# One block for first FFN and projection, transposes moved into the fourth lookup unit, split indices, and the second FFN's first norm spread over the scan

## The chip, the cores and the metric

The kernel runs on one core of a Trainium2 chip. The metric is the device time in microseconds of one execution, the median of several runs. Beside it stands one profiled execution, with its own time and span.

## The reference

A macaron layer on x of 2048 tokens by 256 channels, fp32: half an FFN, a Mamba-2 block, half an FFN.

```
x = x + 0.5 * ffn(layernorm(x))
x = x + mamba(layernorm(x))
x = x + 0.5 * ffn(layernorm(x))
```

The FFN (both times the same weights) takes its three matrices from a table of 16 values by index: `w = lut[idx]` for gate and up (688 x 256) and down (256 x 688), then `silu(gate) * up` and down. The Mamba block is

```
proj = h @ in_proj_w * mup            # z 512, xBC 768, dt 64
xBC  = silu(conv4(xBC) + conv_b)      # causal, 4 taps, by channel
dt   = softplus(dt + dt_bias); dA = exp(-dt * exp(A_log))
state = state * dA + dtx (x) B;  y = C . state   # 2048 steps, 64 heads of 8, state 128
y = (y + D * x); out = rmsnorm(y) * norm_w * silu(z) @ out_proj_w
```

## The kernel before

Tokens are cut in 16 tiles of 128; four tiles make a group (`GT`, `GROUPS` = 4). fp32 products are made of three float32r matmuls of high and low parts (`split_mm`, L68 to L70). There are three stages, each written as a block in which the five engines have their own programs; at a block's end all engines wait for each other.

**build_front** first makes the FFN's weights. A unit is a quarter of the gate and up indices (64 rows, the low table entries' masks on partitions 0 to 63 and the high ones' on 64 to 127, 1408 columns). For each of seven entry pairs VectorE compares the indices with the entry (`mask_d`, L256), ScalarE makes the eighth mask, and TensorE multiplies each mask by a diagonal of table values, three matmuls over 512, 512 and 384 columns (`lookup`, L420), eight masks adding up to the weights in PSUM, which ScalarE copies out (`evac`). Four such units (`QTR`) are followed by six for the down matrix (`low_d`, 512 columns), interleaved with the first group's FFN. The masks of the down units share memory with those of the first four, so VectorE starts them when the fourth unit's last lookup is done (`aused_ok`). Index DMAs are issued on SP's queue (partitions 0 to 63) and on ScalarE's (64 to 127), a quarter each; SP then issues the activations (`x_res`), the down indices and the projection's weights (`win_raw`, `wout_raw`).

The layer norm is the class **Norm**: VectorE computes statistics of a group (`dve_stats`: four `bn_stats`, four `bn_aggr`, one add of eps), GpSimd the inverse root by `pow` (`pool_rstd`, tile `n_rstd`), VectorE the normalised rows (`dve_xn`, tile `n_xn`), TensorE eight transposes (`pe_transpose`, L529), ScalarE the high and VectorE the low parts (`act_hi`, `dve_lo`, tile `n_xT`). For group 0 the statistics stand on VectorE behind the third unit's masks, the rows behind two masks of the fourth, and the transposes on TensorE between third and fourth unit.

Then come four groups of FFN: hidden chunks, then `product` sums into `f_down`, and VectorE adds the result to `x_res` (L317). In the meantime GpSimd subtracts to get the low parts of the projection's weights (`win`, L231) and, at the end, of the output weights (`wout`, L239). The latter stand behind three `pool_rstd` in its queue; the last of these waits for the statistics of group 2 of the projection's norm.

**build_in_proj** is the projection, by group in 11 chunks, six matmuls each, into four PSUM banks `pj` (the memory of the FFN's gate and up banks). ScalarE copies a chunk out (`pre`, `cv`, `zs`), VectorE does three convolution taps for each of six chunks (L643), GpSimd carries the last columns over. `cv`, `zs`, `xbd`, `w` and the others of `mamba_t` lie where the first FFN's weights and raw indices were. VectorE's program begins with the scaling of `conv_w` and `norm.dve_stats(dve, LAST)`.

**build_scan** has 18 steps: in step c it prepares tile c, multiplies tile c-1 and finishes tile c-2 (names a, b_, z; `do_a`, `do_b`, `do_z`). On VectorE a step is, in this order: `xdt` (L1151), `yf`, `u`, `ssum`, two masked products (`mmat`, L1127), the parts of `y` and `state`, a third `mmat`, the update of `x_res` by the output product (L1234, which waits for GpSimd's root `rstd_y`), `y` (L1239) and a fourth `mmat`. GpSimd computes `gs`, `tmp`, `uh`, the weighted inputs `w` (L1274) and `rstd_y`. TensorE's segment products are `seg` (L859, L864), its transposes of `y` L954. At the 48th `yf` (tile 11) SP issues the DMAs that read the FFN's weights back from DRAM. The norm of the second FFN's group 0 stands at the end: statistics of group 0 behind step a = 14, its root on GpSimd at the end of that step, the rows behind step 15 (a = `LAST`); the statistics of group 1 stand inside the last step (z = `LAST`), between the second and third hidden chunk of the FFN's first group.

Of the kernel before, what the change touches and what calls it, by code (L numbers as in the profile page):

```python
# [19 lines left out]
F32 = mybir.dt.float32  # L20
# [105 lines left out]
def build_front(nc, T, A, norm):  # L126
# [3 lines left out]
    with ExitStack() as ctx:  # L130
        sb = lambda n, s, d=F32: ctx.enter_context(nc.sbuf_tensor(n, s, d))
        ps = lambda n, s: ctx.enter_context(nc.psum_tensor(n, s, F32))
        sem = lambda n: ctx.enter_context(nc.semaphore(n))
# [6 lines left out]
        W = GUC * P  # L140
        with ExitStack() as first:
            big = lambda n: first.enter_context(nc.sbuf_tensor(n, [P, W], F32R))
            mask_d, mask_a = [big(f"mask_d{n}") for n in range(GU_D)], [big(f"mask_a{n}") for n in range(GU_A)]
# [10 lines left out]
            "vec_in", "x0_in", "x_in", "win_in", "wout_in", "gu_in0", "gu_in1", "gu_in2", "gu_in3"))  # L154
        dn_in, ident_ok, half_ok, entry_ok, zeroed, hz, two_ok, lut_ok, table_ok = map(sem, (
# [4 lines left out]
            "gate_ok", "up_ok", "silu_ok", "h_ok", "h_hi", "h_lo", "down_ok", "res_ok", "stored"))  # L160
        win, wout, wgu, wd, x_res = T["win"], T["wout"], T["wgu"], T["wd"], T["x_res"]
# [36 lines left out]
        def _(pool):  # L198
# [26 lines left out]
            for k in range(KC):  # L225
# [3 lines left out]
                for part in range(4):  # L229
                    c = slice(part * PCH * P // 4, (part + 1) * PCH * P // 4)  # L230
                    pool.tensor_tensor(win[:, 1, k, :, :].rearrange("p c n -> p (c n)")[:, c], win_raw[:, k, c],  # L231
                                       win[:, 0, k, :, :].rearrange("p c n -> p (c n)")[:, c].bitcast(F32), ALU.subtract)
            norm.pool_rstd(pool, GROUPS)
            norm.pool_rstd(pool, GROUPS + 1)
            norm.pool_rstd(pool, GROUPS + 2)
            pool.wait_ge(h_lo, GROUPS * FCH)
            pool.wait_ge(split_hi, KC + 1)
            for k in range(4):
                pool.tensor_tensor(wout[:, 1, k, :], wout_raw[:, k, :], wout[:, 0, k, :].bitcast(F32), ALU.subtract)  # L239

        @block.vector
        def _(dve):
            def masks(unit, first=1, end=PAIRS):
                for p in range(first, end):
# [5 lines left out]
                    else:  # L250
# [4 lines left out]
                        src = dn_idx[:, 2 * d:2 * d + halves, :].rearrange("p a c -> p (a c)")  # L255
                    dve.tensor_scalar(dst, src, entry[:, p:p + 1], None, ALU.is_equal).then_inc(mask_ok, 1)  # L256
# [15 lines left out]
            norm.dve_start(dve)  # L272
            for unit in range(QTR - 1):
# [46 lines left out]
        def _(act):  # L320
            for q in range(QTR):
# [32 lines left out]
            act.wait_ge(entry_ok, 2 * PAIRS + 4)  # L354
            for unit in range(2):
# [1057 lines left out]
```

## Time and profile before

| | us |
|---|---|
| median of 3 runs | 511.39 |
| lowest, highest run | 511.18, 514.34 |
| profiled execution, its time | 512.58 |
| its span | 510.7 |
| TensorE busy | 470.6 (92%) |
| VectorE busy | 375.0 (73%) |
| ScalarE, GpSimd busy | 280.0, 160.1 |

Terms of the profile: PE is TensorE (PEld its weight loads), DVE VectorE, ACT ScalarE, POOL GpSimd, SP SyncE. A row of the timeline has its start, its length, the engine, the line of the kernel, the operation with output and inputs, and the number merged in it. In brackets behind it stands how long the engine had been idle and what ended that; "issue" is a wait for nothing that the profile shows. `PEq` is TensorE's sequencer. PEclk is the granted clock of TensorE, 1.00 for 2.4 GHz and 0.50 for 1.2 GHz.

### The profile page before, as it was taken

The numbers are of one execution on the slowest core, as the hardware profiler recorded it, in microseconds if no ns is written. First come the engines' busy times: TensorE is split into PE (matmuls) and PEld (weight loads), VectorE is DVE, ScalarE is ACT, GpSimd is POOL, SyncE is SP. The second block draws the span as 40 slices with busy tenths as digits, with TensorE's granted clock in tenths as the row PEclk, the third lists the DMA queues.
The fourth block names the chain that finished last, engine by engine and source line by source line (L and its number), as shares of the span: only waits on it lengthen the run. The fifth ranks groups of instructions, "written<-read, shape, count | busy, mean of one in ns | idle before, by whom it ended". The sixth has DMA issues, their size and how long they took to land.

```text
span 510.7 us, 17071 instructions
## 1 busy us (share of the span) xinstructions
PE 470.6 (92%) x7454; PEld 396.2 (78%) x7454; DVE 375.0 (73%) x745; ACT 280.0 (55%) x505; POOL 160.1 (31%) x215
## 2 busy tenths in 40 slices
PE   3979999999989999888899999999978999999997
PEld 3766798888888787766787788878857778898987
DVE  6977954656678999975788888888759766556443
ACT  3639644344327899998566656666545433323241
POOL 1010032203023111116666667667546310000000
PEclk9979999999999999899999999999989999999999
DMA  8940052000000000010000000000530000100001
GB/s 215 258 187 1 0 227 124 0 3 0 1 0 1 2 1 0 22 42 4 5 5 4 4 6 4 6 4 6 190 167 5 4 1 0 42 20 22 22 21 41
DMA packets 7226, 21.29 MB, mean 42 GB/s; under 512 B 752, under 2 KB 5360, under 8 KB 6512
## 3 DMA queue, kind: packets, MB, share of 16 engines
q1 hardware_dynamic: 6752, 18.05, 10.4%
q10 hardware_dynamic: 400, 2.16, 1.7%
q8 instruction: 58, 0.95, 0.8%
q14 instruction: 16, 0.13, 0.1%
HBM read 12.87 MB, written 6.55 MB: 38 GB/s over the span
## 4 chain that ended last, share of the span: by engine, by line
PE 37%; issue 7%; ACT 4%; POOL 3%; DVE 3%; POOLq 0%; DVEq 0%; ACTq 0%
PE intra L886 5%; PE seg L864 3%; PE yo L1008 2%; POOL w L1274 2%; PE seg L859 1%; PE XB L938 1%; PE new L989 1%; PE yo L954 1%; PE XB L974 1%; PE yo L1011 1%; PE prior L984 1%; PE XB L68 1%; PE yo L70 1%; PE yo L69 1%; PE yo L68 1%
## 5 line engine op out<-in xcount | busy, mean ns | idle before, releaser
L1274 POOL TENSOR_TENSOR w<-xdt,ends 32x512 f32<-32x512 f32 (+3 forms) x63 | 66.5, 1073 | 3.7 <-ACT seg L1035 2.3
L643 DVE SCALAR_TENSOR_TENSOR cv<-pre,vec,cv 128x512 f32<-128x512 f32 x72 | 52.9, 750 | 2.5 <-ACT cv L684 0.8
L514 POOL TENSOR_TENSOR n_rstd<-n_ve,m_half 128x4 f32<-128x4 f32 x12 | 13.0, 1086 | 125.7 <-DVE n_ve L509 125.6
L1035 ACT ACTIVATE seg<-seg 128x512 f32<-128x512 f32 x64 | 35.9, 579 | 29.2 <-PE seg L864 29.1
L1127 DVE TENSOR_TENSOR mmat<-seg,gs 128x512 f32<-128x512 f32 x64 | 42.4, 685 | 9.3 <-ACT seg L1035 8.9
L68 PE MATMUL pj<-n_xT,win 128*128 128x512 f32 x88 | 35.3, 401 | 4.8 <-ACT cv L684 2.4
L864 PEld LDWEIGHTS seg<-abk,m_seg 96*32 96x32 bf16 x2048 | 20.7, 96 | 24.2 <-DVE mmat L1127 13.7
L1048 ACT ACTIVATE f_hT<-f_h 128x512 fp32r<-128x512 f32 (+1 forms) x24 | 15.2, 632 | 40.2 <-DVE f_h L1138 40.2
L70 PE MATMUL pj<-n_xT,win 128*128 128x512 f32 x88 | 34.8, 395 | 0.0
L864 PE MATMUL seg<-abk,m_seg 96*32 96x64 bf16 x2048 | 27.0, 195 | 8.4 <-issue 5.6
L69 PE MATMUL pj<-n_xT,win 128*128 128x512 f32 x88 | 34.6, 393 | 0.0
L1297 POOL TENSOR_TENSOR uh<-u,uh 128x512 fp32r<-128x512 f32 x16 | 21.0, 1312 | 42.0 <-ACT uh L1089 40.2
L378 ACT ACTIVATE f_hT<-f_h 128x512 fp32r<-128x512 f32 (+1 forms) x24 | 15.2, 632 | 34.5 <-DVE f_h L297 34.4
L1142 DVE TENSOR_TENSOR f_hT<-f_h,f_hT 128x512 fp32r<-128x512 f32 (+1 forms) x24 | 16.6, 692 | 16.8 <-ACT f_hT L1048 16.8
L301 DVE TENSOR_TENSOR f_hT<-f_h,f_hT 128x512 fp32r<-128x512 f32 (+1 forms) x24 | 16.5, 689 | 14.0 <-ACT f_hT L378 14.0
L256 DVE TENSOR_SCALAR mask_d<-gu_idx,entry 128x1408 fp32r<-128x1408 int32 x28 | 24.4, 948 | 2.3 <-DMA gu_idx<-in_gu 2.3
L374 ACT ACTIVATE f_sg<-f_gate 128x512 f32<-128x512 f32 (+1 forms) x24 | 14.1, 587 | 19.2 <-PE f_gate L70 19.1
L68 PEld LDWEIGHTS pj<-n_xT,win 128*128 128x128 f32 x88 | 16.7, 189 | 9.4 <-ACT cv L684 3.8
L68 PE MATMUL f_down<-wd,f_hT 128*128 128x256 f32 x80 | 23.0, 288 | 0.3 <-ACT wd L351 0.3
L69 PE MATMUL f_down<-wd,f_hT 128*128 128x256 f32 x80 | 22.7, 283 | 0.0
L70 PE MATMUL f_down<-wd,f_hT 128*128 128x256 f32 x80 | 22.6, 283 | 0.0
L1165 DVE SCALAR_TENSOR_TENSOR yf<-cv,vec,yo 128x128 f32<-128x128 f32 x64 | 18.0, 343 | 5.2 <-PE yo L954 5.2
(266 smaller groups left out, 1448.7 us busy)
## 6 DMA issues: line engine op xcount, KB each, us to landing
wgu_dram<-wgu SPq DMA_DIRECT2D x1, 2816.0 KB, 8.2
wgu<-wgu_dram SPq DMA_DIRECT2D x1, 2816.0 KB, 10.5
out<-x_res SPq DMA_DIRECT2D x8, 256.0 KB, 2.1
x_res<-in_x SPq DMA_DIRECT2D x1, 1536.0 KB, 22.5
wd_dram<-wd SPq DMA_DIRECT2D x1, 1536.0 KB, 11.6
wd<-wd_dram SPq DMA_DIRECT2D x1, 1536.0 KB, 13.6
gu_idx<-in_gu ACTq DMA_DIRECT2D x4, 352.0 KB, 8.3
gu_idx<-in_gu SPq DMA_DIRECT2D x4, 352.0 KB, 9.5
```

The costliest lines, as they stand in the source:

```text
L68: pe.matmul(out, w_hi, x_hi, start=start, stop=False)
L69: pe.matmul(out, w_hi, x_lo, start=False, stop=False)
L70: return pe.matmul(out, w_lo, x_hi, start=False, stop=stop)
L256: dve.tensor_scalar(dst, src, entry[:, p:p + 1], None, ALU.is_equal).then_inc(mask_ok, 1)
L643: dve.scalar_tensor_tensor(dst, pre[:, x, k:k + GN].rearrange("p (t c) -> p t c", c=P), cw[:, x, k:k + 1], dst, ALU.mult, ALU.add).then_in ...
L864: ins = pe.matmul(out[Q * b:Q * b + Q, i, :], T["m_seg"][:, IU * (n - 1) + i, :], T["abk"][:, b, a, :], start=True, stop=True)
L886: ins = pe.matmul(intra[Q * g:Q * g + Q, :, hh, :], mmat[b_ % 2][:, :, h], xbd[b_ % 2][:, h, :, :], start=True, stop=True)
L1035: act.activation(seg[u_ % 2][:, :, :], seg[u_ % 2][:, :, :], ACT.Exp).then_inc(s["exp_ok"], 1)
L1127: dve.tensor_tensor(mmat[a % 2][:, i, :], seg[u_ % 2][:, :, :], gs[a % 2][:, i].unsqueeze(2).broadcast_to([P, IU, HEADS]), ALU.mult).then_ ...
L1165: dve.scalar_tensor_tensor(yf[:, P * g:P * g + P].rearrange("p (b t) -> p b t", b=NB), cv[:, z, g, :].rearrange("p (b t) -> p b t", b=NB), ...
L1274: pool.tensor_tensor(heads(w[r, n, :]), heads(xdt[a % 2][r, :]), ends[a % 2][r, n * HEADS:(n + 1) * HEADS].unsqueeze(2) .broadcast_to([Q * ...
L1297: pool.tensor_tensor(uh[:, 1, :, :].rearrange("p g t -> p (g t)"), u[:, :], uh[:, 0, :, :].bitcast(F32).rearrange("p g t -> p (g t)"), ALU ...
```

## The change

- The block that holds the first FFN also holds the projection. Where the block's end separated them, the projection's VectorE, ScalarE and GpSimd programs wait at their start for all that reads the memory that they write (`ffn1_places`: the last `down_ok`, all subtractions, the weights' stores to DRAM), and TensorE waits for `win`. GpSimd's `wout` subtractions now stand ahead of the last `pool_rstd` of the front.
- The first unit's indices come in two pieces, of 512 and 896 columns, on both queues. VectorE makes the first 512 columns of three masks from the first piece; TensorE waits for both parts of each such mask.
- Group 0's transposes stand behind three of the fourth unit's eight lookups.
- The second FFN's statistics of group 0 are done one tile a step (steps 6 to 9, the end in step 10), those of group 1 in steps 11 to 14 with the end in step 15, the rows of group 0 one tile a step in steps 12 to 15. All of these stand between the third `mmat` and the update of `x_res`. GpSimd's root for group 0 moves from step 14 to step 11.

```diff
@@ build_front
+        T["ffn1_read"] = ((down_ok, GROUPS * GT // 2), (split_lo, 4 * KC + 4), (stored, 32))
+        T["ffn1_banks"], T["win_parts"] = (res_ok, GROUPS * GT // 2), ((split_hi, KC), (split_lo, 4 * KC))
-        block = ctx.enter_context(nc.Block())
@@ sync
-            sp.dma_start(gu_idx[0:H64, 0, :], A["gu"][:, 0, :]).then_inc(gu_in[0], 16)
+            sp.dma_start(gu_idx[0:H64, 0, 0:GN], A["gu"][:, 0, 0:GN]).then_inc(gu_first, 16)
+            sp.dma_start(gu_idx[0:H64, 0, GN:], A["gu"][:, 0, GN:]).then_inc(gu_in[0], 16)
@@ gpsimd
             norm.pool_rstd(pool, GROUPS)
             norm.pool_rstd(pool, GROUPS + 1)
-            norm.pool_rstd(pool, GROUPS + 2)
             pool.wait_ge(h_lo, GROUPS * FCH)
             pool.wait_ge(split_hi, KC + 1)
             for k in range(4):
-                pool.tensor_tensor(wout[:, 1, k, :], wout_raw[:, k, :], wout[:, 0, k, :].bitcast(F32), ALU.subtract)
+                pool.tensor_tensor(wout[:, 1, k, :], wout_raw[:, k, :], wout[:, 0, k, :].bitcast(F32), ALU.subtract
+                                   ).then_inc(split_lo, 1)
+            norm.pool_rstd(pool, GROUPS + 2)
@@ vector
+                    if unit == 0 and p < FIRST:
+                        dst, src = dst[:, GN:], src[:, GN:]
...
+            dve.wait_ge(gu_first, 32)
+            for p in range(1, FIRST):
+                dve.tensor_scalar(mask_d[p - 1][:, 0:GN], gu_idx[:, 0, 0:GN], entry[:, p:p + 1], None, ALU.is_equal
+                                  ).then_inc(mask_first, 1)
@@ scalar
-            for q in range(QTR):
+            act.dma_start(gu_idx[H64:P, 0, 0:GN], A["gu"][:, 0, 0:GN]).then_inc(gu_first, 16)
+            act.dma_start(gu_idx[H64:P, 0, GN:], A["gu"][:, 0, GN:]).then_inc(gu_in[0], 16)
+            for q in range(1, QTR):
@@ tensor
+                        if n < FIRST - 1:
+                            pe.wait_ge(mask_first, n + 1)
                         pe.wait_ge(mask_ok, n + 1)
...
-            for unit in range(QTR):
+            for unit in range(QTR - 1):
                 lookup(unit)
-                if unit == 2:
-                    norm.pe_transpose(pe, 0)
+            lookup(QTR - 1, 0, 3)
+            norm.pe_transpose(pe, 0)
+            lookup(QTR - 1, 3)
             lookup(QTR)
@@ build_in_proj
-        block = ctx.enter_context(nc.Block())
+        def ffn1_places(engine):
+            for read, count in T["ffn1_read"]:
+                engine.wait_ge(read, count)
...
         def _(dve):
+            ffn1_places(dve)
...
         def _(pool):
             norm.pool_rstd(pool, LAST)
+            ffn1_places(pool)
...
         def _(act):
             act.wait_ge(w_ok, 1)
+            ffn1_places(act)
...
         def _(pe):
             x_hi, x_lo = norm.xT[:, 0], norm.xT[:, 1]
+            for parts, count in T["win_parts"]:
+                pe.wait_ge(parts, count)
...
                 if (g, c) == (B4, 1):
                     pe.wait_ge(norm.lo_ok, 2 * GROUPS * KC + KC)
+                    pe.wait_ge(*T["ffn1_banks"])
@@ build_scan, vector (STATS = 6)
                     dve.wait_ge(h_lo, 2)
-                    norm.dve_stats(dve, 1)
...
                 if do_a:
                     masked(a, 3)
+                if STATS <= a < STATS + GT:
+                    norm.dve_stats_of(dve, 0, a - STATS)
+                if a == STATS + GT:
+                    norm.dve_stats_end(dve, 0)
+                if STATS + GT < a <= STATS + 2 * GT:
+                    norm.dve_stats_of(dve, 1, a - STATS - GT - 1)
+                if a == STATS + 2 * GT + 1:
+                    norm.dve_stats_end(dve, 1)
+                if LAST - GT < a <= LAST:
+                    dve.wait_ge(norm.rstd_ok, 1)
+                    norm.dve_xn_of(dve, 0, a - LAST + GT - 1)
...
-                if a == LAST - 1:
-                    norm.dve_stats(dve, 0)
-                if a == LAST:
-                    norm.dve_xn(dve, 0)
@@ build_scan, gpsimd
-                if a == LAST - 1:
+                if a == STATS + GT + 1:
                     norm.pool_rstd(pool, 0)
```

`dve_stats_of` is one `bn_stats`, `dve_stats_end` the four `bn_aggr` and the add, `dve_xn_of` one tile of `dve_xn`.

## Rows read from the trace of the kernel before

**Rows 1.** The page, parts 1 (busy, share, instructions) and 3 (queue, packets, MB).
```profile
PE 470.6 (92%) x7454; PEld 396.2 (78%) x7454; DVE 375.0 (73%) x745; ACT 280.0 (55%) x505; POOL 160.1 (31%) x215
...
q8 instruction: 58, 0.95, 0.8%
```
**Rows 2.** Windows: length, busy us (instructions) by engine, PEclk, DMA share, GB/s.
```profile
154.00:171.00 17.00, 17.00 (x80) 14.16 (x80) 15.75 (x30) 14.34 (x25) 5.54 (x7) 1.00 0.00 1
254.00:364.00 110.00, 105.52 (x3752) 88.75 (x3754) 92.11 (x188) 69.57 (x135) 75.29 (x83) 1.00 0.02 5
412.00:430.00 18.00, 17.18 (x98) 14.04 (x97) 12.78 (x32) 7.13 (x14) 3.19 (x3) 1.00 0.01 1
```
**Rows 3.** Timeline of VectorE in the front.
```profile
6.69 18.21 DVE L256 TENSOR_SCALAR mask_d<-gu_idx,entry 128x1408 fp32r<-128x1408 int32 x21 [2.30 <-DMA gu_idx<-in_gu]
...
26.86 1.82 DVE L256 TENSOR_SCALAR mask_d<-gu_idx,entry 128x1408 fp32r<-128x1408 int32 x2
...
30.05 4.40 DVE L256 TENSOR_SCALAR mask_d<-gu_idx,entry 128x1408 fp32r<-128x1408 int32 x5
...
39.22 5.71 DVE L256 TENSOR_SCALAR low_d<-dn_idx,entry 128x512 fp32r<-128x512 int32 x13 [3.58 <-PE f_down L420]
```
**Rows 4.** Timeline of TensorE: transposes, then lookups 2, 3, 7, 8 of unit four.
```profile
30.19 1.12 PE L529 MATMUL new<-ident,n_xn 128*128 128x128 f32 x4 [3.68 <-DVE n_xn L521]
...
33.13 0.63 PE L420 MATMUL f_up<-mask_d,table 128*128 128x512 f32 x1
...
34.30 0.63 PE L420 MATMUL f_up<-mask_d,table 128*128 128x512 f32 x1
...
37.69 0.39 PE L420 MATMUL f_up<-mask_d,table 128*128 128x512 f32 x1
...
38.32 0.40 PE L420 MATMUL f_up<-mask_a,table 128*128 128x512 f32 x1
```
**Rows 5.** Window of the fourth unit, PEclk 0.50.
```profile
30.00:36.00 6.00, 5.81 (x19) 5.14 (x20) 5.64 (x8) 1.09 (x2) 0.00 (x0) 0.50 0.27 96
```
**Rows 6.** Timeline at the end of the first FFN and the block's end.
```profile
145.48 0.69 DVE L301 TENSOR_TENSOR f_hT<-f_h,f_hT 48x512 fp32r<-48x512 f32 x1 [0.70 <-ACT f_hT L378]
...
150.69 2.78 POOL L239 TENSOR_TENSOR wout<-wout_raw,wout 128x256 fp32r<-128x256 f32 x4
...
151.30 0.28 PE L123 MATMUL f_down<-wd,f_hT 128*128 128x256 f32 x1
...
153.81 0.47 PE L68 MATMUL pj<-n_xT,win 128*128 128x512 f32 x1 [2.23 <-PEq L130]
...
156.80 0.75 DVE L643 SCALAR_TENSOR_TENSOR cv<-pre,vec,cv 128x512 f32<-128x512 f32 x1 [0.64 <-ACT cv L684]
```
**Rows 7.** Waits from 254 to 364 us: who for whom, total us, times, longest.
```profile
DVE x_res L1234 <- POOL rstd_y L1308: 10.3, 10, 1.6
PEld seg L864 <- DVE mmat L1127: 8.9, 10, 1.0
...
PEld seg L864 <- issue: 4.7, 16, 0.8
```
**Rows 8.** Timeline of VectorE from the end of step 14.
```profile
387.14 1.39 DVE L503 BATCH_NORM_STATS2 n_stats<-x_res 128x6 f32<-128x256 f32 x4
...
389.20 0.69 DVE L1151 TENSOR_TENSOR xdt<-XB,dt_tok 128x512 f32<-128x512 f32 x1
...
399.24 1.38 DVE L521 TENSOR_SCALAR n_xn<-x_res,n_mv,n_rstd 128x256 f32<-128x256 f32 x4
...
417.48 1.41 DVE L503 BATCH_NORM_STATS2 n_stats<-x_res 128x6 f32<-128x256 f32 x4
```
**Rows 9.** Timeline of TensorE in step 15.
```profile
389.94 1.08 PE L974 MATMUL XB<-state,cv 128*32 128x128 f32 x32 [1.35 <-DVE xdt L1151]
...
393.48 0.42 PE L864 MATMUL seg<-abk,m_seg 96*32 96x64 bf16 x32 [0.75 <-DVE mmat L1127]
```
**Rows 10.** All roots of the norms on GpSimd: ns min/median/max.
```profile
L514 POOL TENSOR_TENSOR n_rstd<-n_ve,m_half x12: 1006/1018/1617, 27.1 to 466.6; 128x4 f32<-128x4 f32 x12
```
**Rows 11.** Timeline of TensorE while the weights are read back.
```profile
374.12 0.29 PE L864 MATMUL seg<-abk,m_seg 96*32 96x64 bf16 x7 [3.29 <-issue]
```

More of the change, by code:

```diff
@@ L123, in down_mm, with build_front @@
     return pe.matmul(out, hT[:, 0, c, tok], wd[:, 1, c, :], start=False, stop=True)
-def build_front(nc, T, A, norm):
+def build_front(nc, T, A, norm, block, sem):
     with ExitStack() as ctx:
@@ L140, in build_front @@
         W = GUC * P
+        FIRST = 4
         with ExitStack() as first:
@@ L502, in dve_stats, with dve_stats_of, dve_stats_end @@
         for t in range(GT):
-            dve.bn_stats(self.stats[:, t, :], self.rows(g, t)).then_inc(self.stat_ok, 1)
+            self.dve_stats_of(dve, g, t)
+        self.dve_stats_end(dve, g)
+    def dve_stats_of(self, dve, g, t):
+        dve.bn_stats(self.stats[:, t, :], self.rows(g, t)).then_inc(self.stat_ok, 1)
+    def dve_stats_end(self, dve, g):
         dve.wait_ge(self.stat_ok, (g + self.base) * GT + GT)
@@ L520, in dve_xn, with dve_xn_of @@
         for t in range(GT):
-            dve.tensor_scalar(self.xn[:, t, :], self.rows(g, t), self.mv[:, g % GROUPS, t, 0:1],
-                              self.rstd[:, g % GROUPS, t:t + 1], ALU.subtract, ALU.mult).then_inc(self.xn_ok, 1)
+            self.dve_xn_of(dve, g, t)
+    def dve_xn_of(self, dve, g, t):
+        dve.tensor_scalar(self.xn[:, t, :], self.rows(g, t), self.mv[:, g % GROUPS, t, 0:1],
+                          self.rstd[:, g % GROUPS, t:t + 1], ALU.subtract, ALU.mult).then_inc(self.xn_ok, 1)
     def pe_transpose(self, pe, g):
@@ L545, in pe_ready, with build_in_proj @@
         pe.wait_ge(self.lo_ok, (g + self.base) * KC + kc + 1 + KC)
-def build_in_proj(nc, T, norm):
+def build_in_proj(nc, T, norm, block, sem):
     with ExitStack() as ctx:
         sb = lambda n, s, d=F32: ctx.enter_context(nc.sbuf_tensor(n, s, d))
-        sem = lambda n: ctx.enter_context(nc.semaphore(n))
+        stage_sem = sem
+        sem = lambda n: stage_sem("pj_" + n)
         norm.base = GROUPS
@@ L1358, in build @@
             put(win_s, ("win", [P, 2, KC, PCH, P], F32R), side="right")
-            with ExitStack() as ffn1:
-                put(ffn1, *ffn_w)
-                build_front(nc, T, A, norm)
+            sem = lambda n: win_s.enter_context(nc.semaphore(n))
             mamba = ExitStack()
-            put(mamba, *mamba_t)
-            T["abk_in"], T["blank"] = (mamba.enter_context(nc.semaphore(n)) for n in ("abk_in", "blank"))
-            for name in ("intra", "yo"):
-                T[name] = mamba.enter_context(nc.psum_tensor(name, [P, INTER], F32, side="right"))
-            build_in_proj(nc, T, norm)
+            T["abk_in"], T["blank"] = (base.enter_context(nc.semaphore(n)) for n in ("abk_in", "blank"))
+            with nc.Block() as block:
+                with ExitStack() as ffn1:
+                    put(ffn1, *ffn_w)
+                    build_front(nc, T, A, norm, block, sem)
+                put(mamba, *mamba_t)
+                for name in ("intra", "yo"):
+                    T[name] = mamba.enter_context(nc.psum_tensor(name, [P, INTER], F32, side="right"))
+                build_in_proj(nc, T, norm, block, sem)
         build_scan(nc, T, norm2, out)
```

8 lines of the change are left out of this document (6 added, 2 removed).

## The prediction, made before the changed kernel had run

> **What bounds the kernel now.** I read the page first: TensorE is busy for 92% of the span, so no other engine is the bound on average, but an average hides stages [rows 1]. So I read the windows by stage next. In the projection TensorE shows 17.00 of 17 us and VectorE 15.75, in the scan 105.52 of 110 us; at the seam between scan and second FFN TensorE still idles 0.82 of 18 us [rows 2]. Then I went to the places that the diff touches, in the timeline. The reader should see four losses there. At the start VectorE sits idle for 2.30 us until the first indices land, then makes 21 masks without a pause [rows 3]. TensorE then idles 3.68 us for the normalised rows (`n_xn`), and works at the lower clock afterwards [rows 4, 5]. Between first FFN and projection it idles 2.23 us at the end of the block [rows 6]. In the scan's last steps it waits for VectorE, which is computing statistics [rows 8, 9].
>
> **Split indices.** Three masks of 512 columns are now made from the first piece while VectorE would idle, and the three masks behind them have 896 columns. A 1408-column mask comes every 0.87 us (18.21/21), a 512-column one every 0.44 us (5.71/13) [rows 3], so 896 columns cost 0.43 and a column 0.48 ns. The three small masks (3 x 0.44 = 1.3 us) fit in the idle 2.30 us if the first piece lands by 5.4 us. Each later mask is 512 x 0.48 ns = 0.25 us shorter: VectorE runs 0.7 us ahead from then on. Two DMA issues more, one on SP and one on ScalarE's queue; behind them stand the later index pieces and the activations' rows, which the same 21 masks keep VectorE from wanting. Bounds: 0 (the first piece lands with the second) and 0.75. I take 0.7, since the second piece ends at the same byte of each queue as before. TensorE still waits for both pieces before its first matmul, so it starts only 0.25 us earlier; the 0.7 counts only further on.
>
> **Transposes inside the fourth unit.** Before, TensorE met the transposes with nothing behind them that it could do. Now it first does three of the fourth unit's eight lookups. Masks one and two exist at once; mask three is the first of the five at 30.05, ready at 30.05 + 0.87 = 30.9, less 0.7 is 30.2 [rows 3]. A lookup (three matmuls) takes 38.32 - 37.69 = 0.63 us at the full clock and 34.30 - 33.13 = 1.17 at the lower one; the eight transposes took 1.6 us at the lower clock (30.19 to the next lookup near 31.8), so 0.8 at the full one [rows 4, 5]. If the clock stays up: 30.2 + 0.63 + 0.8 = 31.6, then five lookups; but the last mask is ready at 34.45 - 0.7 = 33.75, and two lookups follow it: 35.0. Before, the unit ended at 38.32 + 0.63 = 38.95. Gain 4.0 us. It includes the 0.7 above. Does the clock stay up? The one long gap of 3.68 us (26.5 to 30.19) becomes two: from 26.5 - 0.7 = 25.8 to mask one at 26.86 + 0.87 - 0.7 = 27.0, 1.2 us, and from mask two's lookup (27.9 + 0.63 = 28.5) to mask three at 30.2, 1.7 us. The clock did not fall behind the 2.23 us gap between the blocks [rows 6], so I take it that it holds. If it falls, TensorE restarts at the same 30.2 as before at 1.2 GHz and gets 2.4 GHz back near 36 as before [rows 5]: 30.2 + 1.17 + 1.6 = 33.0, two and a half lookups until 36, the rest in 1.6: 37.6, a gain of 1.4. What follows hangs on the unit's end: VectorE's next masks waited 3.58 us for it [rows 3]. VectorE's low parts of the transposes now end near 34.9, just ahead of it.
>
> **One block.** The block's end waited for GpSimd, whose four `wout` subtractions ran to 150.69 + 2.78 = 153.5 behind an `n_rstd` [rows 6]; they now stand ahead of that `n_rstd`, wait only for the last group's `h_lo` (145.48 + 0.69 = 146.2), and end 2.78 later, at 149. TensorE's first projection matmul can follow the last product (151.30) by its pitch, near 151.45 instead of 153.81: 2.36 us. TensorE's own new wait (`win_parts`) is for splits that stand in GpSimd's queue ahead of three `n_rstd` and of these subtractions, so they are long done. ScalarE and VectorE wait for the last product (`down_ok`), near 151.6; the first chunk takes 1.6 us of TensorE anyway. VectorE carries the projection (15.75 of 17 us [rows 2]): its first convolution tap stood at 156.80 behind ScalarE's `cv` [rows 6] and moves with TensorE, but its residual to 152.3, the coefficients and 2.1 us of statistics (as in [rows 8]) stand ahead and end at 154.6. So 2.2 us. Bounds: 1.5 (only its idle time at the barrier) and 2.36.
>
> **Statistics strewn.** Removed from step 15's head: nine instructions, 387.14 to 389.20, 2.06 us [rows 8]. TensorE waited 1.35 us for `xdt`, which stands behind them, and then 0.75 for `mmat`, which it waits for in every step (8.9 us in ten steps) [rows 7, 9]. VectorE runs without a gap there, so its whole chain moves, save what TensorE's transposes of `y` hold back: 1.9. Removed behind step 15: four `n_xn`, 1.38 us. TensorE has matmuls of its own there, so between 0 and 1.3; I take 0.4, nearer to 0, because no gap of TensorE on them stands among the rows. Removed from the last step: 2.04 us of statistics at 417.48 [rows 8]; TensorE idles only 0.82 us in that stretch, most of it ahead of them [rows 2]; between 0.3 and 0.8, I take 0.5. Together 2.8.
> Added to steps 6 to 15: eight statistics of 1.39/4 = 0.35, two ends of 2.06 - 1.39 = 0.67, four `n_xn` of 0.35: 5.5 us. They stand ahead of the update of `x_res`, where VectorE waited for GpSimd's root 10.3 us in ten steps, 1.03 each [rows 7]. One insertion a step hides in it; steps 12 to 14 carry two (0.70) and step 15 an end and an `n_xn` (1.02), which may slip by 0.3. GpSimd's `n_rstd` (1.02 us, [rows 10]) moves from step 14, where `gs` of step 15 stood behind it, to step 11, where its inputs exist. The root's median is 1018 ns, but 1617 ns once, when masks (tensor_scalar) ran beside it [rows 3, 10]. So an `n_xn`, also tensor_scalar, may hold GpSimd's small root: at most its own 0.35 a step, 1.4 in four. I take 0.2. Cost 0.5, net 2.3.
> The Trainium skill (SBUF — State Buffer, Who interferes with whom) says that VectorE and GpSimd share a port pair as a lock held for a whole instruction, and names tensor_scalar among those that take it. By that rule the four `n_xn` cost up to their full length in a row that GpSimd wants just then, and the net would be 1.1 instead of 2.3; the one long root agrees with it.
>
> **Sum.** 4.0 + 2.2 + 2.3 = 8.5. The profiled execution took 512.6 (span 510.7): 504.1. It lay 1.2 above the median of the runs, 511.4: **502.9**.
>
> **Rivals.**
> - *The clock falls in the front all the same*: 1.4 instead of 4.0: 505.5. For it: the stretch before is under three quarters busy, as lookups of 0.63 wait for masks at 0.87, and two gaps stand close together. Against: no gap is as long as 2.23. 0.28.
> - *The strewn work is not hidden*: all 5.5 on the path instead of 0.5: 507.9. For it: the scan is a loop between TensorE and VectorE (0.9 us of wait for `mmat` a step), so a slipped `y` or `xdt` reaches both. Against: the slot of 1.03. 0.13.
> - *Code loading moves*: queue q8 brought 58 packets for 7454 matmuls with as many weight loads, one per 257 instructions [rows 1]. TensorE showed 4.7 us of "issue" waits before `seg` in 110 us, 16 times, the longest 0.8 [rows 7]; 3752 matmuls there need 29 packets. The new program shifts where packets end. If all 29 stalled it 0.8 us, that is +18.5: 521, slower than before; it decides from 0.46 us a packet (4.7 + 8.5 over 29). Nothing points that way: 0.03.
> - *The stall under the weights' load goes*: once the "issue" wait was 3.29 us, while the FFN's weights were read back [rows 11]. If packets fall luckily it goes: 499.6. 0.10.
> - The forecast, all three parts and the clock held: 0.46.
>
> **Range.** From 499.5 (the last rival) to 507.0 (the clock falls and the insertions cost 1.5 more). Outside lie half of the hidden-work rival, the code loading and part of the last: 0.15. A measurement here tells 1%, about 5 us, from no change: faster is below 506.3. The forecast, the fallen clock, the missing stall and a quarter of the strewn rival: 0.87; within 1%: 0.10; slower: 0.03.
>
> **What would show it.** In the changed profile: TensorE's gap before the transposes split in two and the fourth unit over by 35; granted clock 1.00 between 29 and 36. Projection matmuls directly behind the last product, no block end between. No wait of TensorE for `xdt` in step 15; VectorE's wait before `x_res` down from 1.03 to about 0.6 in steps 6 to 15, with 105 us or more of matmuls in 110 us of the scan as before. Wrong if the share falls below 94%, if the clock's low stretch stays, or if the convolution taps start less than 1.5 us closer to the last product.

## The result, and the profile after

The changed kernel took 507.37 us (median of 4 runs, 502.74 to 508.81), the kernel before on the same chip 512.87 (4 runs): ratio 0.9867, 95% interval 0.9825 to 0.9909, or 6.8 us less (4.7 to 9.0). Measured again later beside other kernels (7 runs against 11) it was 504.48 against 514.03: 0.9827 (0.9782 to 0.9872), or 8.9 us less. The forecast was 8.5 less. Its absolute 502.9 started from the 511.4 of the runs shown, and the first chip's 507.37 lies 0.4 above its range; against the kernel before on the same chip both measurements are about where it said.

The profiled execution took 508.81 (span 506.9) against 512.58 (510.7), only 3.8 less. Its page, parts 1 and 3, shows that TensorE's work is unchanged and that q8, which brings the code, has the same 58 packets:

```profile
PE 470.8 (93%) x7454; PEld 397.5 (78%) x7454; DVE 375.3 (74%) x748; ACT 279.7 (55%) x505; POOL 161.0 (32%) x215
...
q8 instruction: 58, 0.95, 0.8%
```

The timeline of VectorE gives marks that cut the run into stages (start, length, ..., idle time before and its releaser):

```profile
4.66 1.28 DVE L283 TENSOR_SCALAR mask_d<-gu_idx,entry 128x512 fp32r<-128x512 int32 x3 [0.38 <-DMA gu_idx<-in_gu]
7.91 4.47 DVE L264 TENSOR_SCALAR mask_d<-gu_idx,entry 128x896 fp32r<-128x896 int32 x6 [1.97 <-DMA gu_idx<-in_gu]
...
154.53 0.75 DVE L677 SCALAR_TENSOR_TENSOR cv<-pre,vec,cv 128x512 f32<-128x512 f32 x1
...
359.24 0.68 DVE L1191 TENSOR_TENSOR xdt<-XB,dt_tok 128x512 f32<-128x512 f32 x1
374.74 0.68 DVE L1191 TENSOR_TENSOR xdt<-XB,dt_tok 128x512 f32<-128x512 f32 x1
387.05 0.68 DVE L1191 TENSOR_TENSOR xdt<-XB,dt_tok 128x512 f32<-128x512 f32 x1
```

| stage, between marks of VectorE | before | after | change | forecast |
|---|---|---|---|---|
| start to the first low-part mask (`low_d`) | 39.22 | 39.39 | +0.2 | -4.0 |
| to the first convolution tap | 117.58 | 115.14 | -2.4 | -2.2 |
| to `xdt` of step 0 | 70.45 | 70.49 | 0.0 | 0 |
| to `xdt` of step 13 | 134.01 | 134.22 | +0.2 | +0.5 |
| to `xdt` of step 14 | 14.42 | 15.50 | +1.1 | 0 |
| to `xdt` of step 15 | 13.52 | 12.31 | -1.2 | -1.9 |
| to VectorE's last instruction | 118.26 | 116.63 | -1.6 | -0.9 |

The sum is -3.8. Most of what is missing is in the first row. There the 896-column masks start at 7.91, where the whole masks started at 6.69 [rows 3]. TensorE's timeline in the fourth unit:

```profile
28.38 0.47 PE L437 MATMUL f_up<-mask_d,table 128*128 128x512 f32 x1 [1.47 <-DVE mask_d L264]
...
31.47 0.80 PE L437 MATMUL f_up<-mask_d,table 128*128 128x512 f32 x1 [1.41 <-DVE mask_d L264]
...
32.81 1.05 PE L556 MATMUL new<-ident,n_xn 128*128 128x128 f32 x4
...
38.48 0.40 PE L437 MATMUL f_up<-mask_a,table 128*128 128x512 f32 x1
```

The 3.68 us gap [rows 4] did become two short ones, 1.47 and 1.41, as the forecast had it (1.2 and 1.7). But the granted clock was 0.50 from 30.8 for 6.8 us; each four transposes took 1.05 us, as at the lower clock before, and the eighth lookup starts at 38.48, where it started at 38.32 [rows 4]. At the seam the timeline shows no gap at all: the last product at 151.36, the first projection matmul 0.12 later (before: 151.30 and 153.81 [rows 6]).

```profile
151.36 0.28 PE L123 MATMUL f_down<-wd,f_hT 128*128 128x256 f32 x1
...
151.48 0.40 PE L68 MATMUL pj<-n_xT,win 128*128 128x512 f32 x1
```

While the FFN's weights are read back, TensorE now stood still twice, where it stood once before ([rows 11], 3.29):

```profile
367.16 0.58 PE L926 MATMUL intra<-xbd_even,mmat 128*32 128x32 f32 x25 [2.10 <-issue]
...
373.18 0.30 PE L904 MATMUL seg<-abk,m_seg 96*32 96x64 bf16 x8 [1.77 <-issue]
```

The windows (length, busy us by engine, PEclk, DMA share, GB/s) show the two places at the lower of TensorE's levels, and the scan's main stretch with 0.9 us less TensorE work (104.67 against 105.52, with 102 fewer matmul records) and 2 us more VectorE than in [rows 2]:

```profile
30.00:38.00 8.00, 6.59 (x22) 5.71 (x22) 6.16 (x9) 1.08 (x2) 0.00 (x0) 0.57 0.19 66
364.00:379.00 15.00, 11.13 (x325) 9.97 (x328) 7.60 (x17) 4.40 (x10) 5.98 (x8) 0.66 0.62 259
...
254.00:364.00 110.00, 104.67 (x3650) 86.86 (x3638) 94.15 (x198) 69.58 (x135) 75.34 (x83) 1.00 0.04 10
```

And the waits from 254 to 364 us: VectorE's wait ahead of `x_res` is down from 10.3 us in ten steps [rows 7] to 7.4 in nine, TensorE's wait for VectorE's `mmat` as it was (8.9 before).

```profile
PEld seg L904 <- DVE mmat L1167: 8.7, 10, 1.0
DVE x_res L1284 <- POOL rstd_y L1354: 7.4, 9, 1.4
...
PEld seg L904 <- issue: 4.5, 15, 0.7
```

### The profile page after: what moved, and what is told of

The parts are those of the page before. It is cut to its first block, busy times and chain, and to the rows that moved or that the text cites. A ratio compares the mean times of both kernels' runs of the same rounds, so it can differ in the third digit from the quotient of the medians.

```text
span 506.9 us, 17072 instructions
## 1 busy us (share of the span) xinstructions
PE 470.8 (93%) x7454; PEld 397.5 (78%) x7454; DVE 375.3 (74%) x748; ACT 279.7 (55%) x505; POOL 161.0 (32%) x215
## 4 chain that ended last, share of the span: by engine, by line
PE 47%; issue 3%; DVE 3%; ACT 3%; DVEq 0%; ACTq 0%
PE intra L926 6%; PE seg L904 4%; PE yo L1048 3%; PE XB L1014 2%; PE new L1029 2%; PE XB L978 2%; PE seg L899 2%; PE yo L994 2%; PE prior L1024 2%; PE yo L1051 1%; PE XB L68 1%; PE XB L70 1%; PE XB L69 1%; PE BG L68 1%; DVE mmat L1167 1%
## 5 line engine op out<-in xcount | busy, mean ns | idle before, releaser
L538 POOL TENSOR_TENSOR n_rstd<-n_ve,m_half 128x4 f32<-128x4 f32 x12 | 13.5, 1123 | 110.0 <-DVE n_ve L533 109.9
L1088 ACT ACTIVATE f_hT<-f_h 128x512 fp32r<-128x512 f32 (+1 forms) x24 | 15.2, 632 | 38.1 <-DVE f_h L1178 38.1
L393 ACT ACTIVATE f_hT<-f_h 128x512 fp32r<-128x512 f32 (+1 forms) x24 | 15.2, 632 | 34.4 <-DVE f_h L309 34.3
L1182 DVE TENSOR_TENSOR f_hT<-f_h,f_hT 128x512 fp32r<-128x512 f32 (+1 forms) x24 | 16.6, 691 | 16.8 <-ACT f_hT L1088 16.8
L313 DVE TENSOR_TENSOR f_hT<-f_h,f_hT 128x512 fp32r<-128x512 f32 (+1 forms) x24 | 16.6, 690 | 14.0 <-ACT f_hT L393 14.0
L264 DVE TENSOR_SCALAR mask_d<-gu_idx,entry 128x1408 fp32r<-128x1408 int32 (+1 forms) x28 | 23.6, 921 | 2.0 <-DMA gu_idx<-in_gu 2.0
L926 PE MATMUL intra<-xbd_even,mmat 128*32 128x32 f32 x1024 | 19.4, 225 | 2.9 <-issue 2.7
## 6 DMA issues: line engine op xcount, KB each, us to landing
wd<-wd_dram SPq DMA_DIRECT2D x1, 1536.0 KB, 13.9
```

The lines of the kernel that those rows point to most:

```text
L313: dve.tensor_tensor(low_part(hT, c, r), h[0:r, :], hT[0:r, 0, c, :].bitcast(F32), ALU.subtract).then_inc(h_lo, 1)
L926: ins = pe.matmul(intra[Q * g:Q * g + Q, :, hh, :], mmat[b_ % 2][:, :, h], xbd[b_ % 2][:, h, :, :], start=True, stop=True)
```

## The experiments

Every kernel ran beside the kernel before on the same chip: four against 35 of its runs (514.40 median), four against 11 (512.80), four against 11 (514.03). Differences are the ratio times that median. The granted clock of each execution is recorded too; from its mean follows how long TensorE was at 1.2 GHz. In the kernel before that was 16.6, 18.5 and 15.7 us on average in the three groups; in the second, one execution's record alone says 66 us, and without it the average is 13.7.

### The parts alone

The first four are the kernel before with one part of the diff each. Block alone:

```diff
-        block = ctx.enter_context(nc.Block())
...
+            with nc.Block() as block:
+                with ExitStack() as ffn1:
+                    put(ffn1, *ffn_w)
+                    build_front(nc, T, A, norm, block, sem)
```


> Before plus the merged block alone (front and projection in one block, the output-weight subtractions ahead of the last root). In the changed kernel's profile the first projection matmul came 2.33 us earlier after the same fourth-unit time. Theory A (the seam's gain carries to the end, as VectorE carries the projection): 2.2 us faster than before, about 0.5%. Rival (the gain is given back in the scan, because code packets and the clock shift): under 1 us.

Measured 509.82: 0.9914 (0.9887 to 0.9942), 4.4 us less. In its trace the stage from low-part mask to tap took 115.08, 2.5 less, and the stages behind it are within 0.4 us of before. The stage ahead of it took 38.03 instead of 39.22, though its instructions are those of the kernel before: the clock was low in the fourth unit for 3.4 us here and for 6.8 there. Its executions had 12.1 us at 1.2 GHz, 4.5 less than the kernel before beside it, worth up to 2.2. The term of 2.2 holds.

Transposes alone:

```diff
+            lookup(QTR - 1, 0, 3)
+            norm.pe_transpose(pe, 0)
+            lookup(QTR - 1, 3)
```


> Before plus the transposes behind three of the fourth unit's eight lookups, indices whole. The changed kernel gained nothing here: its clock fell all the same and its second index piece landed 1.2 us later. Theory A (the late piece ate it): without the split the fourth unit ends 1.3 us earlier with the clock fallen, 3.3 us earlier where it holds. Rival (the transposes' place is worth nothing by itself, since the last masks set the unit's end): under 0.5 us.

Measured 512.30: 0.9972 (0.9937 to 1.0007). That is 1.4 us less, with an interval that includes no change. In its profiled execution the clock was low for 6.8 us from 30.0, and the low-part masks start at 38.72, only 0.5 earlier: nearer to the rival than to the 1.3 expected for a fallen clock.

Statistics alone:

```diff
-                    norm.dve_stats(dve, 1)
+                if STATS <= a < STATS + GT:
+                    norm.dve_stats_of(dve, 0, a - STATS)
```


> Before plus the strewn statistics alone. Theory A (hidden in VectorE's wait before the x_res update): 2.3 us faster. Theory B (part of it is on the path: the starts of steps 6 to 10 lost 1.4 us against before in the changed profile): gains 2.8 to 3.3 at the end, loses 1.4 to 2, so 1 to 1.5 us faster, and the starts of xdt in steps 6 to 10 drift by over 1 us against before.

Measured 510.73: 0.9913 (0.9882 to 0.9944), 4.5 less, more than either expectation. The trace doesn't show where it comes from, as its execution (513.78) is the slowest of the twelve: step 14 to 15 took 12.3 (before 13.5), from step 15 to the end 116.8 (118.3), but step 13 to 14 took 16.6 (14.4), since TensorE waited 3.19 and 2.47 for issue there, and steps 0 to 13 took 135.8 (134.0). The drift of over 1 us in steps 6 to 10 is not there: 43.2 against 42.8.

Split alone:

```diff
-            sp.dma_start(gu_idx[0:H64, 0, :], A["gu"][:, 0, :]).then_inc(gu_in[0], 16)
+            sp.dma_start(gu_idx[0:H64, 0, 0:GN], A["gu"][:, 0, 0:GN]).then_inc(gu_first, 16)
+            sp.dma_start(gu_idx[0:H64, 0, GN:], A["gu"][:, 0, GN:]).then_inc(gu_in[0], 16)
```


> Before plus the index pieces alone. Theory A (the second piece of SP's queue now lands behind ScalarE's next quarter, so masks start at 7.9 instead of 6.7): 0.4 us slower than before, the first full mask near 7.9. Rival (the late landing in the changed profile was chance): first full mask near 6.7 and 0.7 us faster.

Measured 513.66: 0.9988 (0.9948 to 1.0029). VectorE waited even longer than in the changed kernel and than expected (its full masks start at 9.67, not near 7.9), and the low-part masks came 2.1 us late (41.34):

```profile
4.20 1.27 DVE L280 TENSOR_SCALAR mask_d<-gu_idx,entry 128x512 fp32r<-128x512 int32 x3
9.67 2.74 DVE L261 TENSOR_SCALAR mask_d<-gu_idx,entry 128x896 fp32r<-128x896 int32 x4 [4.21 <-DMA gu_idx<-in_gu]
```

The four measured gains, 4.4, 1.4, 4.5 and 0.6, add up to 10.9 us, 2 to 4 more than the whole change gave. Each is uncertain by about 1.5 to 2 us, and the traces don't say what the excess is.

### Why the split gave nothing

No split (the changed kernel with quarter 0 in one piece):

```diff
-            sp.dma_start(gu_idx[0:H64, 0, 0:GN], A["gu"][:, 0, 0:GN]).then_inc(gu_first, 16)
-            sp.dma_start(gu_idx[0:H64, 0, GN:], A["gu"][:, 0, GN:]).then_inc(gu_in[0], 16)
+            sp.dma_start(gu_idx[0:H64, 0, :], A["gu"][:, 0, :]).then_inc(gu_in[0], 16)
```


> The changed kernel with quarter 0 of the indices in one piece again (block, transposes and strewn statistics stay). Theory now: the split gained nothing, because in the changed kernel the second piece landed later than the whole quarter did before; so the front alone gets 0.3 to 0.6 us shorter without it (the low-part masks of VectorE start near 38.7 to 39.0 instead of 39.39), and the time is that of the changed kernel or up to 0.7 less. Rival, the term of the prediction: the split was worth 0.7 us, the low-part masks start near 40.1 and the time is 0.7 us longer. In either case TensorE's granted clock falls inside the fourth unit.

Measured 505.93: 0.9870 (0.9825 to 0.9914), that is, level with the changed kernel. But the part of the expectation that the clock falls in either case is refuted: in this execution it didn't. Its TensorE idles 1.46 and 1.40 us as the changed kernel's does, then runs the unit at full speed, and VectorE's low-part masks start at 36.12, 3.1 us earlier than before:

```profile
36.12 1.16 DVE L259 TENSOR_SCALAR low_d<-dn_idx,entry 128x512 fp32r<-128x512 int32 x2 [0.50 <-PE f_down L423]
```
```profile
30.00:38.00 8.00, 5.96 (x29) 4.57 (x29) 7.50 (x13) 3.01 (x6) 0.52 (x1) 1.00 0.22 79
```

Ordered pieces (the changed kernel; quarter 1 goes out when both pieces of quarter 0 have landed):

```diff
+            sp.wait_ge(gu_in[0], 32)
             for q in range(1, QTR):
                 sp.dma_start(gu_idx[0:H64, q, :], A["gu"][:, q, :]).then_inc(gu_in[q], 16)
...
+            act.wait_ge(gu_in[0], 32)
             for q in range(1, QTR):
                 act.dma_start(gu_idx[H64:P, q, :], A["gu"][:, q, :]).then_inc(gu_in[q], 16)
```


> The changed kernel, both pieces kept, but SyncE and ScalarE issue quarter 1 of the indices only when both pieces of quarter 0 have landed. Theory: the second piece was late because the next quarter's bytes shared the DMA engines with it; with nothing behind it it lands by about 6.2 us, the 896-column masks start by 6.5 instead of 7.91, and the split gives the 0.7 us of the prediction after all (low-part masks near 38.0 to 38.4, 1 us ahead of the changed kernel). Rival: a second transfer costs its own fixed time whatever stands behind it; masks start at 7.5 or later and the front stays at 39.3.

Measured 502.96: 0.9806 (0.9769 to 0.9843). Now the second piece is there in time. Its timeline of VectorE:

```profile
4.42 1.28 DVE L284 TENSOR_SCALAR mask_d<-gu_idx,entry 128x512 fp32r<-128x512 int32 x3
6.23 3.60 DVE L265 TENSOR_SCALAR mask_d<-gu_idx,entry 128x896 fp32r<-128x896 int32 x5 [0.52 <-DMA gu_idx<-in_gu]
```

The DMA issues (KB each, median us from issue to landing) say the same of SyncE's second piece, first in the changed kernel, then here:

```profile
gu_idx<-in_gu SPq DMA_DIRECT2D x1, 224.0 KB, 6.0
```
```profile
gu_idx<-in_gu SPq DMA_DIRECT2D x1, 224.0 KB, 4.4
```

The packets show how. In the kernel before, the last packet of SyncE's part of quarter 0 ended at 5.80, when 10 of the 64 packets of ScalarE's part of quarter 1 were through. In the changed kernel the last packet of SyncE's second piece ended at 6.76, and by then 55 of those 64, and 6 of SyncE's own quarter 1, were through; with the split alone it ended at 8.53, behind 64 and 52. With ordered pieces it ended at 5.50. Which of the two queues' waits matters more was not tried. The Trainium skill (DMA: Bandwidth & Descriptors, Queues, rings and completion order) says that a DMA engine takes turns between the rings that have work, a packet at a time. The counts of packets agree with it. The low-part masks of executions with the clock held start at 36.12 and 36.19 in one piece, and at 35.59 and 35.47 with ordered pieces (the runs of the next sections; here the chained weights and the filled gaps on top of the ordered pieces):

```profile
35.59 3.53 DVE L265 TENSOR_SCALAR low_d<-dn_idx,entry 128x512 fp32r<-128x512 int32 x8 [0.50 <-PE f_down L439]
```
```profile
35.47 3.93 DVE L265 TENSOR_SCALAR low_d<-dn_idx,entry 128x512 fp32r<-128x512 int32 x9 [0.51 <-PE f_down L439]
```

So the split is worth 0.5 to 0.7 us there, once nothing overtakes its second piece: about the 0.7 of the forecast. (In two executions with a low clock of 3.4 us the marks are only 0.1 apart, 37.23 and 37.16.) The run times don't confirm it: the ratio fell by more than 0.7 us explains (0.9870 to 0.9806), the intervals overlap, and the changed kernel measured again, with its late piece, came to 0.9827.

### Whether filled gaps keep the clock up

Filled gaps, on the kernel without the split (nobody reads the fillers' result):

```diff
+            fill(4)
+            lookup(QTR - 1, 0, 2)
+            fill(5)
+            lookup(QTR - 1, 2, 3)
```


> The kernel of the run without the split, and nine extra matmuls of 512 columns whose result nobody reads: four ahead of the fourth unit's first lookup, five ahead of its third, in the two gaps of 1.4 to 1.5 us where TensorE waited for masks. Theory: the clock fell at 30.8 because TensorE stood idle in these gaps; filled, it stays at full speed through the unit, the transposes take 0.8 instead of 1.6 us and each lookup 0.63 instead of 1.17, and the low-part masks start near 36.0, 2.7 us ahead of the run without fillers; time 2 to 3 us less. Rival: the fall goes by something else (the lookups at three quarters' load since 8 us), the clock falls all the same, and the fillers cost up to 1 us.

Measured 503.52: 0.9826 (0.9790 to 0.9863). Clock up in the unit, low-part masks at 36.19; but they stood at 36.12 without fillers. The same on top of the ordered pieces:

> The kernel with the ordered pieces and the nine filler matmuls in the fourth unit's two gaps (their result is read by nobody). In the run of the filled gaps the clock stayed up in the unit, but it also did in one without fillers. Theory: fillers keep it up in each execution; again no low clock between 27 and 38, low-part masks at 35.5 to 36, and a median 1 us below the ordered kernel's. Rival: what TensorE did before counts as much; in some executions the clock falls with fillers too, and nothing is gained.

Measured 503.85: 0.9809 (0.9764 to 0.9853), against 0.9806 without fillers; gaps down to 0.55 and 0.26, clock up again, low-part masks at 35.47. So both executions with fillers held the clock. Eight were profiled with the transposes in the unit and no fillers. All have the same lookups and the same two gaps of 1.4 to 1.5 us, yet TensorE was at 1.2 GHz there for 0 us in two (no split; chained weights, below), for 3.4 in two (ordered pieces; tripled statistics) and for 6.8 in four (the changed kernel both times, transposes alone, paced weights). So the gaps alone don't decide it. It went roughly with the time at which the clock had first risen in that execution: 10.8 and 11.0 in the two without a fall, 12.8 to 13.7 in the four with the long one, but 9.9 and 13.2 in the two between. In the two executions with fillers it had risen at 10.9 and 11.2, beside the two that held without fillers, so these two say little for the fillers. Whether fillers cure it stays open, and the medians (0.9826 with against 0.9870 without, 0.9809 against 0.9806 on the ordered pieces) show no gain for certain.

### The stall under the weights' load

Paced weights, on the kernel without the split: six pieces, one for every two units of the scan.

```diff
-            for name in ("wgu", "wd"):
+            parts = [("wgu", hl, k) for hl in range(2) for k in range(KC)] + [("wd", hl, None) for hl in range(2)]
+            for n, (name, hl, k) in enumerate(parts):
+                sp.wait_ge(s["seg_ok"], UNITS * 13 + 3 + 2 * n)
```


> The kernel of the run without the split; the FFN's weights are read back from DRAM in the scan's step 13 and after in six pieces, one for every two units of the scan, instead of in two transfers issued at once. Theory: TensorE's issue waits of 1.8 and 2.1 us in steps 13 and 14, and the 10 us at 1.2 GHz behind them, come from the weights' bytes holding up q8's packets; paced, no issue wait is above 1 us there, the clock stays, and step 14 lasts 12 us instead of 14.4 to 15.5: 3 to 4 us less. Rival: the stalls belong to q8's packets wherever they fall (the FFN's code is new code), pacing only spreads them: same time within 1 us. A third case: the last piece lands after the second FFN wants it, and the time is longer by what TensorE then waits.

Measured 505.91: 0.9860 (0.9822 to 0.9899), no gain. The stalls stayed, the first under a single 704 KB piece, which takes 4.1 us from issue to landing, the second under two of them, issued 2.8 us apart:

```profile
366.38 0.55 PE L917 MATMUL intra<-xbd_even,mmat 128*32 128x32 f32 x24 [2.36 <-issue]
...
379.36 0.31 PE L917 MATMUL intra<-xbd,mmat 128*32 128x32 f32 x5 [1.43 <-issue]
```

Chained weights, on the ordered kernel: twelve pieces of 320 and 384 KB, each issued when the one before has landed.

```diff
+            for n, (name, hl, k, c) in enumerate(parts):
+                if n:
+                    sp.wait_ge(loaded, 16 * n)
```


> The kernel with the ordered pieces, and the FFN's weights read back in twelve pieces of 256 to 416 KB, each issued when the one before has landed (before: two transfers of 2816 and 1536 KB at once). TensorE's wait for the weights is split: the second FFN's first product waits for all, the first hidden chunk for the eight pieces of wgu. Theory: an issue wait of TensorE lasts as long as bytes of the weights stand ahead of a q8 packet; with at most one small piece ahead no issue wait is above 1.2 us, the 3.4 us of low clock behind it goes, step 13 to 14 takes 11 to 12 us instead of 13.3 to 15.8; 2 to 4 us less than the ordered kernel. Rival: the fetch is held up by any transfer in flight, and the stalls come in small parts with the same sum (3 to 4 us). Third: the chain lasts beyond 400 us, and TensorE waits for wgu there.

Measured 501.33: 0.9759 (0.9713 to 0.9805), beside it on the same chip the changed kernel again:

> The changed kernel once more, nothing altered, as the measure for the three kernels that run beside it. If the gain of the ordered pieces is real, this one is 2 to 4 us slower than the ordered ones (about 0.987 of the kernel before); if it was scatter, they are level. Its front: the 896-column masks start near 7.9 and the low-part masks at 38 to 39.4, and the low clock in the fourth unit lasts 0, 3.4 or 6.8 us, since the same front showed all three.

504.48: 0.9827 (0.9782 to 0.9872). The changed kernel once more stood still twice (3.47 and 1.52) and needed 17.1 us from step 13 to 14. The chained one needed 11.9. (At 510.57 us that profiled execution was the slowest of its seven, 6 us above their median; the averages of stages below leave it out.) The chained kernel's waits from 355 to 380 us list no issue wait above 0.8; the window shows the clock up and 14.02 of 15 us of TensorE work, where the changed kernel had 11.13:

```profile
PEld intra L937 <- issue: 1.5, 2, 0.8
...
PEld seg L915 <- issue: 1.0, 3, 0.6
```
```profile
364.00:379.00 15.00, 14.02 (x498) 11.71 (x497) 12.62 (x27) 9.26 (x19) 9.17 (x11) 1.00 0.37 101
```

No wait for `wgu` appears at its first use near 391 us. Its executions were at 1.2 GHz for 3.7 us on average, the changed kernel's beside it for 8.8, the kernel before for 15.7. The packets of q8 tell why: between 254 and 340 us one came every 3.7 to 3.9 us on average and never later than 4.9 after the last, in every kernel. Under the two transfers there were gaps of 5.9 to 7.4 us, one or two in each trace, and TensorE stood still at the end of each (in the kernel before the gap lasts from 364.3 to 371.7). Under the first seven chained pieces no gap was above 5. (One of 5.9 began at 384.0, across the last piece of wgu and the first of wd, and there TensorE had no issue wait above 0.8.) So the code's packets are held up by the weights' bytes in front of them, and small pieces, one in flight, largely end that. Of the kernels run this has the lowest time: 2.4% under the kernel before, 0.7% under the changed one, and 0.5% under the ordered one on which it stands; both pairs of intervals overlap. Between step 13 and 14 its trace has 3.6 us less than the first trace of the changed kernel, and 1.3 less than that of the ordered one (13.3), which had one stall.

### Whether the strewn statistics are hidden

The kernel without the split, each of the four statistics in steps 6 to 9 done three times:

```diff
+        for n in range(extra):
+            dve.bn_stats(self.xn[:, t, 8 * n:8 * n + 6], self.rows(g, t))
```


> The kernel without the split, and each of the four statistics strewn over steps 6 to 9 done three times (two extra results go to a free tile): eight extra VectorE instructions of 0.35 us, 2.8 us of work in slots that before showed 1.03 us of VectorE waiting each. Theory of the prediction: what stands in the slot is hidden as long as it is under the slot (3 x 0.35 = 1.05), so the sum of steps 6 to 9 stays as without, and the time within 0.5 us. Rival: the slot is not free, the insertions reach the loop between TensorE and VectorE; then steps 6 to 9 grow by 2 to 2.8 us and the time with them, and the changed kernel's own eight statistics and four normalisations cost about as much per instruction.

Measured 506.42: 0.9863 (0.9823 to 0.9904), as without them (0.9870). From step 6 to step 10 it took 43.8 us, in the kernel without the split 44.3. That trace is at the slow end (all others took 42.3 to 44.4, the kernel before 42.8), but 2.8 us on top of any of them would stand out. The waits from 282 to 325 us, first without, then tripled:

```profile
PEld seg L890 <- DVE mmat L1153: 3.0, 4, 0.8
...
DVE x_res L1270 <- POOL rstd_y L1340: 4.6, 4, 1.4
```
```profile
PEld seg L892 <- DVE mmat L1155: 3.0, 4, 0.8
...
DVE x_res L1272 <- POOL rstd_y L1342: 1.6, 3, 0.7
```

The 2.8 us of extra work came out of VectorE's wait (4.6 to 1.6), and TensorE's wait for `mmat` didn't move by a tenth. The slot is real, to its whole length, in steps 6 to 9. The later steps with two insertions and the `n_xn` were not tested this way.

## Why the prediction was right, and where it was not

Its gain of 8.5 lies in both measured intervals, by terms of which some were right and some cancelled. Of its own signs, the projection's matmuls follow the last product directly, TensorE's wait for `xdt` in step 15 is gone, and its share in the scan's stretch is 95%, where below 94 was to be wrong. But the low stretch of the clock stayed, which was a sign of being wrong, the fourth unit wasn't over by 35, and VectorE's wait before `x_res` came to 0.8 us and not 0.6. For the scan I average the stages over the profiled executions: four without strewn statistics (the kernel before, block, transposes, split alone), nine with.

- **One block**: forecast 2.2, 2.5 in the block alone, 2.4 in the changed kernel. TensorE follows by one pitch, and VectorE's tap moves with it. Right.
- **Statistics, step 15's head**: forecast 1.9; step 14 to 15 went from 13.7 to 11.8. Right.
- **Statistics behind it**: forecast 0.4 + 0.5 = 0.9; from step 15 to the end 118.3 became 117.0, 1.2 before rounding. The step "between 0 and 1.3; I take 0.4" was sized low, or the 0.5 was; the runs don't part them.
- **Cost of the strewn work**: forecast 0.5. From step 0 to 13: 135.1 without, 134.0 with, single executions 131.9 to 138.1. With the tripled run: nothing that shows. The 0.2 for the small root was about right: the five roots between 340 and 400 us had a mean of 541 ns before and 580 after, 0.2 in all. Two of them, at 567 and 705 ns, started within 0.15 us of an `n_xn`; the other three took 542, one of these with an `n_xn` beside it for its last quarter of a microsecond. The longest:

```profile
L1354 POOL TENSOR_TENSOR rstd_y<-ve_y,m_half 128x1 f32<-128x1 f32 x5 | 2.9, 580 | 8.5 <-ACT ve_y L1146 8.5
...
384.65 0.70 POOL L1354 TENSOR_TENSOR rstd_y<-ve_y,m_half 128x1 f32<-128x1 f32 x1 [1.17 <-ACT ve_y L1146]
```

That isn't the full length of the `n_xn` (0.35 each, 1.4 in all) that the Trainium skill's lock (SBUF — State Buffer, Who interferes with whom) would have allowed; the measurement decides for 0.2 here.
- **Split indices**: forecast 0.7, measured nothing or a loss. The step that failed is "the second piece ends at the same byte of each queue as before". It does, but more of the next quarter is through before its last packet (55 of the other queue's 64 packets, where it was 10). With order restored, 0.5 to 0.7.
- **The clock in unit four**: "so I take it that it holds" failed as a certainty. It is a matter of the execution: six of eight fell, partly or fully. Where it held, the low-part masks start at 36.12 without the split and 35.59 with ordered pieces, 3.1 and 3.6 earlier than in the trace before, whose clock was low for 6.8 us (forecast 4.0 for both parts; with ordered pieces the third mask's lookup started at 30.50 instead of 30.2). Where it fell for 6.8 us, they start at 38.72 and 38.76 without the split, 0.5 earlier, and at 39.39 with the late piece, 0.2 later. The rival had put 1.4 on it: it took 2.4 GHz to be back near 36 and the restart at 30.2, and the changed kernel restarted at 31.47 and was at 1.2 GHz until 37.6. The inference from the 2.23 us gap between the blocks didn't carry over. TensorE is busy up to that gap, while the lookups ahead of unit four wait for masks; that this makes the difference is argued, not shown.
- **The weights' load**: the forecast kept the one stall of 3.29, the rival let it vanish for luck. With the weights in two transfers, all four profiled executions without strewn statistics had one stall, of 2.7 to 3.3. Of eight with them, five had two (the changed kernel both times, statistics alone, both filled ones) and three had one. Step 13 to 14 took 13.9 on average without and 15.2 with (paced and chained left out), a cost of 1.3 that the forecast lacked. That the moved instructions shift which packets fall under the load is argued, not shown: the ordered kernel has the changed kernel's TensorE program and stalled once, so timing counts too.

Added up from the traces: block 2.5, statistics 1.9 + 1.2, the stall -1.3, the front -0.2 as profiled: 4.1 us with the clock down in the front, and some 2.6 more with it up (36.12 against 38.72), 6.7. The measured 6.8 and 8.9 (intervals 4.7 to 11.2) lie at the upper end of this and above. What may add to it is the clock elsewhere: TensorE was at 1.2 GHz for 9 to 10 us per execution in the changed kernel and 15.7 in the kernel beside its second measurement, worth up to 3.4 us (half of 15.7 - 8.8), a part of which is the front's and counted already. So the total was right partly by luck: a front and a stall worse than forecast were made up for by something that the forecast didn't have. The traces show the same three low places in both kernels (unit four, once near 205 us for 3.4 us, and behind the stall). Why the kernel before is low so much longer on average stays open.

## What to carry to other kernels

A transfer cut in two so that its first part comes sooner can make the second part later, as it did here, unless the transfers behind it, on both queues, are held until it has landed. A bulk transfer in the middle of a phase with much straight-line code is better sent in small pieces, one in flight: in the one trace taken, twelve pieces instead of two ended stalls of 1.3 to 3.7 us each and the low clock behind them. An engine's wait that comes round in every step can be filled to its length with work from a critical place, and tripling that work in a run shows how long the slot is.

## What the hardware showed that was not expected

- Two executions of one instruction sequence with the same two gaps of 1.4 to 1.5 us differed by 6.8 us at 1.2 GHz, and by 2.6 us at the unit's end (36.12 against 38.76, no split against paced weights). The front of the kernel before did so too, by 1.2 us (39.22 against 38.03 with the block alone).
- q8's packets (16 KB each: 0.95 MB in 58) starve behind bulk transfers: TensorE stood still for up to 3.65 us while 2816 and 1536 KB were on their way, for 2.36 us under pieces of 704 KB, and for at most 0.8 us under pieces of 320 and 384 KB issued one by one.
- A 224 KB piece took 4.4 us from issue to landing with nothing behind it, and 6.0 us with the next quarter issued behind it on both queues (7.8 in the run of the split alone).
